# A second attention's software pipeline: the input's maximum a slot later, the quantised input behind the queries' copies, and two cells moved from PSUM to SBUF

## The reference

```python
def _dyn_quant(x):
    s = jnp.maximum(jnp.max(jnp.abs(x), axis=-1, keepdims=True) / 127.0, EPS)
    q = jnp.clip(jnp.round(x / s), -127.0, 127.0)
    return (q, s)
...
    q = _w8a8_linear(x, wq, bq).reshape(B, N, H, D).transpose(0, 2, 1, 3)
    k = (cond @ wk.T + bk).reshape(B, L, H, D).transpose(0, 2, 1, 3)
    v = (cond @ wv.T + bv).reshape(B, L, H, D).transpose(0, 2, 1, 3)
    scores = jnp.einsum('bhnd,bhld->bhnl', q, k) * inv_sqrt_d + mask[:, None]
    attn = jax.nn.softmax(scores, axis=-1)
    o = jnp.einsum('bhnl,bhld->bhnd', attn, v)
    return _w8a8_linear(o, wo, bo)
...
    x = x + jnp.tanh(g_xattn[1]) * _L1_xattn_ref(_layernorm(x, axis=-1), ctx_2048, ...)
    x = x + jnp.tanh(g_ffn[1]) * _L1_ffn_ref(_layernorm(x, axis=-1), ...)
```

## Time and profile before

| | us |
|---|---|
| median of three runs | 1836.82 |
| the three runs | 1828.48 to 1837.65 |
| the profiled execution | 1837.09 |
| its span, first to last instruction | 1835.3 |
| granted TensorE clock over the span | 0.984 |

### The profile page before, as it was taken

One profiled execution on the slowest core, in us unless ns is written; L12 is line 12 of the kernel. 1 busy time (PEld: TensorE's weight loads), 2 busy tenths in 40 slices (PEclk: granted clock), 3 DMA queues, 4 the chain that ended last, 5 costly groups with the idle time before them and its releaser, 6 DMA issues. The chain is left out here.

```text
span 1835.3 us, 28402 instructions
## 1 busy us (share of the span) xinstructions
PE 1727.9 (94%) x10014; PEld 1359.4 (74%) x10052; DVE 1159.5 (63%) x2436; ACT 1047.1 (57%) x2334; POOL 971.2 (53%) x864
## 2 busy tenths in 40 slices
PE   6999999999999999999998999989999878879998
PEld 4788888887877778777776888879999756634444
DVE  5666555557566675567666657644443768868886
ACT  3666666655655556555554421146656467858776
POOL 5654566545654457645531100038888446657774
PEclk9999999999999999999999999999999989999999
DMA  7121111101111111011222100167889770000000
GB/s 255 48 60 52 48 37 60 56 22 52 37 42 45 52 48 51 19 37 53 58 83 99 58 24 24 46 208 222 228 223 269 193 173 1 1 1 24 24 18 29
DMA packets 113611, 141.36 MB, mean 77 GB/s; under 512 B 38000, under 2 KB 68720, under 8 KB 113280
## 3 DMA queue, kind: packets, MB, share of 16 engines
q1 hardware_dynamic: 106304, 122.76, 21.2%
q0 software_dynamic: 7168, 16.78, 4.3%
HBM read 104.91 MB, written 29.36 MB: 73 GB/s over the span
## 5 line engine op out<-in xcount | busy, mean ns | idle before, releaser
L787 POOL TENSOR_TENSOR a_xcl<-xT,a_xch 128x512 fp32r<-128x512 f32 x64 | 86.1, 1346 | 335.4 <-ACT a_xch L571 335.4
L689 DVE TENSOR_REDUCE a_nmax<-a_S 128x1 f32<-128x192 f32 (+3 forms) x256 | 134.8, 548 | 49.3 <-PE a_S L897 49.1
L954 PE MATMUL a_A<-a_pT,a_vf 128*128 128x512 f32 x320 | 164.8, 597 | 0.3 <-ACT a_pT L592 0.3
L577 ACT ACTIVATE a_pr_odd<-a_S,a_nmax 128x320 f32<-128x320 f32 (+1 forms) x128 | 80.5, 630 | 120.5 <-DVE a_nmax L689 119.8
L120 PE MATMUL a_A<-a_wlo,a_xch 128*128 128x512 f32 x256 | 147.0, 574 | 1.2 <-DVE a_qT L685 1.2
L120 PE MATMUL a_S<-xl,xh 128*128 128x288 f32 (+3 forms) x320 | 122.5, 383 | 8.2 <-DVE xl L722 4.1
L2643 PE MATMUL f_HH<-w12T,f_f_xqT 128*128 128x512 bf16 x496 | 117.7, 383 | 10.7 <-DVE f_h L2496 7.8
L1619 POOL TENSOR_TENSOR e_wlo<-expert_raw,e_whi 128x1408 fp32r<-128x1408 f32 x31 | 101.0, 3260 | 50.4 <-ACT e_whi L1832 48.2
L577 ACT ACTIVATE a_pr_even<-a_S,a_nmax 128x192 f32<-128x192 f32 (+1 forms) x128 | 66.6, 523 | 103.5 <-DVE a_nmax L689 103.4
L120 PE MATMUL e_GUP<-e_xgl,e_whi 128*128 128x256 f32 (+1 forms) x384 | 110.7, 288 | 4.7 <-DVE e_xgl L1917 3.2
L714 DVE RECIPROCAL a_rec<-a_rs 128x1 f32<-128x1 f32 x256 | 41.2, 161 | 108.9 <-ACT a_pr_even L577 58.3
(11 more groups left out here) (443 smaller groups left out, 5576.5 us busy)
## 6 DMA issues: line engine op xcount, KB each, us to landing
a_pw<-in_L_ffn_w_dram SPq DMA_DIRECT2D x96, 256.0 KB, 2.8
expert_raw<-in_L_ffn_w_gate_dram SPq DMA_DIRECT2D x16, 704.0 KB, 8.0
expert_raw<-in_L_ffn_w_up_dram SPq DMA_DIRECT2D x16, 704.0 KB, 9.9
expert_raw<-in_L_ffn_w_down_dram SPq DMA_DIRECT2D x16, 512.0 KB, 10.3
tern<-a_tern SPq DMA_DIRECT2D x48, 128.0 KB, 1.7
x_res<-in_x_dram SPq DMA_DIRECT2D x4, 1024.0 KB, 9.1
a_raw<-in_L_xattn_wq_dram SPq DMA_DIRECT2D x4, 1024.0 KB, 5.9
a_raw<-in_L_xattn_wo_dram SPq DMA_DIRECT2D x4, 1024.0 KB, 5.5
```

Source lines behind the costliest of these rows:

```text
L577: act.activation(pr[s % 2][:, i, 0:keys(s)], pair(s, i), ACT.Exp, bias=nmax[:, s % 2, i:i + 1], accum_out=rs[:, s % 2, i:i + 1]).then_inc( ...
L689: ve.tensor_reduce(nmax[:, s % 2, i:i + 1], pair(s, i), AX.X, ALU.max, negate=True).then_inc(s_max, 1)
L787: pool.tensor_tensor(xcl[:, t % 2], xT[:, :, tok(t)], xch[:, t % 2].bitcast(F32), ALU.subtract).then_inc(xlo_ready, 1)
L954: pe.matmul(bank, vf[:, par(t), i], pT[:, i % 2], start=i == 0, stop=False)
```

## The change

It reorders three queues of the second attention and the end of the stage ahead, and moves two cells.

- On VectorE m moves from the end of the slot to behind M and one tile nearer (`AHEAD` 2 instead of 3), and x moves to the end of the slot.
- On ScalarE the queries' copies k move ahead of q, c and v, and q moves from the head of the slot to behind k.
- On TensorE K moves ahead of V0, and T behind Y.
- `am` and `mx` become SBUF cells, and V0's wait on `m_ready` is dropped.
- At the end of the expert stage, the third maximum is dropped (slot 0 has it now), the first `input_copy` moves ahead of the second maximum, and ScalarE's second `quantise_input` behind the first queries' scaling.

```diff
                 centre(1)
                 quantise_input(0)
-                quantise_input(1)
                 copy_weight(4)
-                centre(2)
                 act.wait_ge(q_full, 1)
                 act.wait_ge(m_ready, 2)
                 act.activation(qs[:], QY[:], ACT.Identity, scale=sx[:, 0]).then_inc(qs_ready, 1)
+                quantise_input(1)
+                centre(2)
                 act.wait_ge(q_turned, 1)
...
                 values(0)
+                input_copy(0)
                 maximum(1)
                 statistics(2)
-                input_copy(0)
                 values(1)
...
                 input_copy(1)
-                maximum(2)
                 copy_weight(7)
...
-    PE_ORDER = "S0 U0 P0 Q0 P1 V0 K0 T0 V1 Y0"
+    PE_ORDER = "S0 U0 P0 Q0 P1 K0 V0 V1 Y0 T0"
-    ACT_ORDER = "q0 t0 i0 t1 c0 v0 k0 e0 O0"
+    ACT_ORDER = "t0 i0 t1 k0 q0 c0 v0 e0 O0"
-    DVE_ORDER = "D0 o0 M0 b0 x0 N0 Y0 m0"
+    DVE_ORDER = "D0 o0 M0 m0 b0 N0 Y0 x0"
...
-             "DVE": {"b": 3, "m": 3, "x": 2, "D": 0, "M": 0, "N": -1, "o": -2, "Y": -2},
+             "DVE": {"b": 3, "m": 2, "x": 2, "D": 0, "M": 0, "N": -1, "o": -2, "Y": -2},
...
-    ACT_JOIN = {10: "q0.12 t0.9 i0.11 t1.9 c0.13 v0.13 k0.11 G0.0 e0.10 O0.9",
+    ACT_JOIN = {10: "t0.9 i0.11 t1.9 k0.11 q0.12 c0.13 v0.13 G0.0 e0.10 O0.9",
...
-                13: "q0.15 t0.12 i0.14 t1.12 fc0.0 fv0.0 k0.14 e0.13 O0.12",
-                14: "t0.13 i0.15 t1.13 fc0.1 fv0.1 k0.15 e0.14 O0.13 fq0.0 fq1.0",
+                13: "t0.12 i0.14 t1.12 k0.14 q0.15 fc0.0 fv0.0 e0.13 O0.12",
+                14: "t0.13 i0.15 t1.13 k0.15 fc0.1 fv0.1 e0.14 O0.13 fq0.0 fq1.0",
...
-    DVE_JOIN = {13: "D0.13 o0.11 M0.13 fb0.0 x0.15 N0.12 Y0.11",
+    DVE_JOIN = {13: "D0.13 o0.11 M0.13 m0.15 fb0.0 N0.12 Y0.11 x0.15",
...
-        am, mx, amo, mo = O[:, 0, STAT:STAT + 2], O[:, 1, STAT:STAT + 2], O[:, 2, STAT:STAT + 2], O[:, 3, STAT:STAT + 2]
+        am, mx, amo = homes["am"], homes["mx"], O[:, 2, STAT:STAT + 2]
...
                         if s > 0:
                             pe.wait_ge(o_ready, s)
-                        if n == 0 and s + 3 < NT:
-                            pe.wait_ge(m_ready, 2 * (s + 4))
```

More of the change, by code:

```diff
@@ L2775, in turn_weights @@
                 sp.wait_ge(turned, 96)
-            homes = {**attention1_ffn1_homes(nc, kept, weights, sb), **{n: front[n] for n in ("cx", "xq", "xqT", "qs", "qT", "stats", "mv", "var", "root", "unroot", "rec", "sx")}}
+            homes = {**attention1_ffn1_homes(nc, kept, weights, sb), **{n: front[n] for n in ("cx", "xq", "xqT", "qs", "qT", "stats", "mv", "var", "root", "unroot", "rec", "sx", "am", "mx")}}
             attention1_ffn1_stage(nc, x, x_loaded, ident, gates, wT, sq, bq, gsw, gbo, mask, kbd, vbd, g12, g3, w12T, w3T, at, out, turn_weights, homes, front_sems)
```

## The result

The changed kernel takes 1839.74 us (median of 20 runs, 1831.62 to 1841.16) against 1835.23 us of the kernel before (20 runs, 1828.48 to 1837.89): a ratio of 1.0024, 95% interval 1.0015 to 1.0034. It is 0.24% slower, where 1832.2 with a range of 1824 to 1838 had been forecast. The profiled execution spans 1838.0 us against 1835.3, and its time is 1839.8 against 1837.1.

A forecast was written before the change was run, and what follows sets the result against it. A dependency ring over three engines was taken to set the 8.37 us slot. Stage end -2.6, slots 2 to 9 -3.0 and slots 10 to 13 +1.0 sum to -4.6 us, giving 1832.2 us, range 1824 to 1838.

The forecast's parts named there:

- a ring over three engines: Ordinary slot of the second attention before: a dependency ring over ScalarE, TensorE and VectorE sums to 8.37 us, exactly the slot.
- the ring through x and U: Ordinary slot after: U, i, K, V0, V1, N, Y, x, back to U sum to 8.01 us; -3.0 us over eight slots.
- ring (b): Ordinary slot after: the quantised output O follows N, and U stands behind O; 8.00 us.
- Reads of a 128x1 cell: Cells am and mx moved to SBUF: reads change by hundredths of a us, priced at nothing.
- the first rival: VectorE becomes the bound and the clock rises: slots of 7.90, -8.3 us, 1828.5 us in all; chance 0.2.
- VectorE's queue (a): Ordinary slot after: VectorE's own queue without idle, 8.37 - 0.47 = 7.90 us; bound of -3.8 us for the slots.
- the rule of the most contended engine: Skill rule taking the highest-occupancy engine for the bound: VectorE, 90% busy, would set slots of 7.90, sum 0.9 us lower.
- Slots 10 to 13: Extra ScalarE steps ahead of e delay O and U: three slots of 8.77, one of 8.01; +1.0 us, bounds 0 and +2.
- The end of the expert stage: Earlier first input copy (1.45) and dropped third maximum (1.16) start the next stage earlier: -2.6 us, bounds -1.2 and -2.9.
- The first two slots: Start of the second attention, where TensorE's clock is granted at 0.50: no change taken, bounds -1.9 and +0.4 us.
- The slower rival: U waits for x in slots 2 to 13; a hand-over of 0.80 gives +2.1 us, 1839 us in all; chance 0.08.

The follow-up runs named there:

- the orders alone: The changed kernel with am and mx back in O's PSUM bank and V0's wait on m_ready back, all orders as changed: 1845.33 us, ratio 1.0057 to before.
- the steps behind O: The changed kernel with one-operand sx and early tile 2 statistics, plus G0, H0 and H1 behind the quantised output O: 1829.58 us, ratio 0.9966 to before.
- the last two experiments: Changed kernel with one-operand sx, early tile 2 statistics, and G0, H0, H1 behind O: 1829.58 us; the same with x ahead of Y on VectorE: 1821.57 us.

## Why the prediction was wrong

*The slot is set by a ring over three engines.* Right. With the second operand gone, the slot follows the ring through x and U, 8.15 for 8.01, and with x moved it follows ring (b), 7.92 for 8.00.

*"Reads of a 128x1 cell change by hundredths of a us, off the ring below: nothing."* This is the step that failed, and the larger of the two. For the reads themselves it holds: mx's own calculation takes 0.23 from PSUM (in the experiment with the orders alone) and 0.21 from SBUF. But in one of the instructions that read them, sx, both tensor operands lie in SBUF after the move, and that one then waits for GpSimd: 0.20 to 1.04 in the slots, 0.84 on VectorE's queue, where N's idle could cover about half of it: 8.51 in place of 8.15. In the trace of before sx with both tensors in SBUF runs only at the end of the expert stage, where it shows almost nothing: 0.25 once beside GpSimd's square roots, and 0.20 twice beside an idle GpSimd.

```profile
1461.03 0.25 DVE L1976 SCALAR_TENSOR_TENSOR front_sx<-front_mx,front_unroot,front_floor 128x1 f32<-128x1 f32 x1
...
1464.25 0.20 DVE L1976 SCALAR_TENSOR_TENSOR front_sx<-front_mx,front_unroot,front_floor 128x1 f32<-128x1 f32 x1
```

Yet the price stood in that trace, in the first attention, where the same operation on 128x512 reads two tensors in SBUF. Its row there (minimum, median and maximum in ns, then first and last start), and one of the 48 with GpSimd's row beside it:

```profile
L711 DVE SCALAR_TENSOR_TENSOR a_tern<-a_pw,a_thr,a_xn x48: 750/815/1518, 413.9 to 940.1; 128x512 bf16<-128x512 f32 x48
```

```profile
441.55 1.52 DVE L711 SCALAR_TENSOR_TENSOR a_tern<-a_pw,a_thr,a_xn 128x512 bf16<-128x512 f32 x1
```

```profile
440.03 2.49 POOL L803 TENSOR_TENSOR a_pr_odd<-a_pr_odd,a_rec 128x576 f32<-128x576 f32 x2
```

24 of the 48 start while GpSimd is at work; they take 0.88 to 1.52, and every one ends 0.55 behind the GpSimd instruction that was running (here 443.07 against 442.52). The other 24 take 0.75.

What would have helped is to ask of each moved operand which engine shares the way to it, and to look at GpSimd's timeline at the new place of the instruction. The prediction costed every queue but GpSimd's, which it took to be held by Y alone. The Trainium skill, page "GPSIMD Engine Reference", section "Specifications", says that GpSimd's SBUF interfaces are shared with VectorE and that instructions of VectorE with two SBUF inputs contend for them; the two ends at 1509.62 and 1509.64 agree with it. Taken as a wait until GpSimd's instruction ends, as the 24 rows above show it, sx could have been priced, as an estimate from its place behind M, at up to the whole subtraction's 1.90.

*The new ring at 8.01.* Nearly right. The hand-over from x to U is 0.14, not the 0.05 that was taken from ScalarE's hand-over to TensorE, and K to V0 is 0.49 instead of 0.45; that makes 8.13 to 8.15. Eight slots would have given 8 x (8.15 - 8.38) = -1.8, not -3.0, had sx not grown.

*VectorE's queue (a) and the rule of the most contended engine.* VectorE did become the bound, which the first rival had said, but at 8.52 and not at 7.90, and with the opposite sign: the rival took its queue from before, and the wait for GpSimd came on top of it. Busy time is no measure of work here: VectorE is busy 8.13 us of a slot with that wait and 7.4 without it (1508.02 to 1516.15 with one operand). In the two kernels without the wait rings set the slot, at 8.15 and 7.92, with VectorE near its limit. The prediction's sign for this rival, no idle left ahead of N, did show. So the rule of the Trainium skill, page "Perfetto Trace Analysis", section "Identifying the Most-Contended Engine", pointed to the right engine in the changed kernel, but none of the slots took the 7.90 that it gave.

*Slots 10 to 13, +1.0.* Right: +1.03, and for the stated reason, as the steps behind O show. N of slot 11 to N of slot 12 is 8.82, forecast 8.77. That the sum fits so well is in part luck: the four pitches are 8.59, 8.82, 8.83 and 8.14, and without the long sx it is +1.26 (34.61 - 33.35).

*The end of the expert stage, -2.6.* The second step that failed. VectorE's part came as worked out (1.45 of waiting gone, the maximum gone, its end 2.57 earlier counted from the first statistics), but what set the stage's start was GpSimd's end plus 7.2 us, and the change itself moved that end 0.4 later. The prediction read VectorE's idle of 2.07 ahead of the memset as a fixed price behind VectorE's end; the row names TensorE's sequencer as its releaser, which is no proof of VectorE's being last. GpSimd's rows at the same place, 1467.14 and 1474.90, would have shown the second path. The bounds given, -1.2 and -2.9, lacked the end at zero.

*The first two slots, 0.* Measured +0.6, a little past the bound of +0.4. One part is sx in slot 0, 1.03 instead of 0.20 (1482.26). With one operand the same stretch took 25.60 us, 1.4 less than before. In that execution the granted clock was 0.90 from 1486.3 to 1488.3, where the changed kernel had 0.50. Which part of that comes from the kernel was not separated.

*The slower rival.* The sign was its, the mechanism was not: it had U waiting 0.80 for x, and the hand-over is 0.14. (By its own terms the sign turns at 0.56, not 0.54.) None of the rivals held a longer instruction on VectorE. And every case, this one too, took the 2.6 us of the stage's end as won, so the range ended at 1838.

*What was left out.* The cells' move and the new order were priced apart. The orders without the move (9.02) show that V0's wait, worth nothing in the old order, is worth 0.5 to 0.9 us a slot in the new one.

## What to carry to other kernels

When an operand moves from PSUM to SBUF, count for each instruction that reads it how many tensor operands then lie in SBUF, and look up what GpSimd is running at that moment; a constant passed as an immediate or a scalar per partition avoids the pair. At a stage border follow each engine's last instruction to its first in the next stage, its DRAIN included: freeing one engine brings only what the next-latest path leaves. A ring worked out from start-to-start pitches gave the slots to 0.15 us wherever the durations stayed as they were, so the durations are what a moved or re-homed instruction has to be checked for first.

## What the runs showed of the hardware

- A 128x1 scalar_tensor_tensor of VectorE with two tensor operands in SBUF ends with the GpSimd tensor_tensor that was running when it started: 1.04 us beside a subtraction of 1.90, 0.41 beside an addition of 1.27, 0.20 with GpSimd idle; beside the 128x1 square roots it took 0.25. A 128x512 one ends 0.55 behind the GpSimd instruction (0.88 to 1.52 us, 24 times) and takes 0.75 where none was running when it started. With one tensor operand in PSUM (0.20), or as a tensor_scalar with one tensor operand (0.195), it isn't held beside the same subtraction.
- At this border between two stages GpSimd took 7.2 us from its last instruction to its first where it came last, 4.98 of them until its DRAIN ended; VectorE took 1.6 where it came last.
- A hand-over to TensorE took 0.14 us from VectorE's end (x to U) and 0.06 from ScalarE's (O to U).
- Equal gaps don't always give the same clock. From N of slot 14 to N of slot 15 TensorE idles 2.13 us once in both of the last two experiments' kernels; the stretch then took 11.48 us at a granted clock of 0.85 (the extra steps behind O) and 9.81 at 1.00 (x ahead of Y). In the ten profiled executions it is 9.81 six times and 11.4 to 11.5 four times. The start of the first statistics differs by about 8 us between executions too, as said above. Both enter the medians, which is why pieces of the trace are compared here and why the gains of the last two experiments can't be read from their medians alone. The cause of this variation stays open.
